# A transformer-gated recurrence on one core: four pieces of a hand-ordered slot change places

## What is computed

```python
x = L0_attn_x
xn = _layernorm(x, axis=-1)
s = recurrence(xn)                 # s_t = A s_{t-1} + B u_t, y = C s + D
g = _silu(_L0_ffn_ref(xn, ...))
return x + s * g

# in _L0_ffn_ref, DEPTH = 6 times:
x = attn_layer(shift_tokens(x), Wqkv[i], q_scale[i], k_scale[i], Wo[i]) + x
x = ffn_layer(shift_tokens(x), ln_g[i], ln_b[i], W1[i], b1[i], W2[i], b2[i]) + x
# attn_layer: 16 heads of 64, q and k l2-normalised and rotated,
# softmax over a local window of 32 (64 keys a query), then Wo
# ffn_layer: layernorm, W1, a * gelu(gate), W2
```

## Time and profile before

| | |
|---|---|
| median of 3 runs | 1641.66 us (1640.87 to 1642.63) |
| the profiled execution, its own time | 1641.48 us |
| its span | 1639.7 us |
| TensorE busy | 1575.6 us, 96% |
| VectorE busy | 1418.0 us, 86% |
| GpSimd busy | 1233.6 us, 75% |
| ScalarE busy | 1113.4 us, 68% |

### The profile page before, as it was taken

One profiled execution on the slowest core, in us unless ns is written; L12 is line 12 of the kernel. 1 busy time (PEld: TensorE's weight loads), 2 busy tenths in 40 slices (PEclk: granted clock), 3 DMA queues, 4 the chain that ended last, 5 costly groups with the idle time before them and its releaser, 6 DMA issues.

```text
span 1639.7 us, 75430 instructions
## 1 busy us (share of the span) xinstructions
PE 1575.6 (96%) x31996; PEld 1314.5 (80%) x31996; DVE 1418.0 (86%) x2750; ACT 1113.4 (68%) x1989; POOL 1233.6 (75%) x1200
## 2 busy tenths in 40 slices
PE   6889999999999999999999999999999999999997
PEld 3577888888888888888888888788888878888885
DVE  5798988898899889889988988998889889888963
ACT  4356667766776777676777767776676676667764
POOL 2677877887787878777887777787778887877851
PEclk9899999999999999999999999999999999999998
DMA  3232223333223333322333322333323333322231
GB/s 113 65 73 69 69 69 96 78 84 83 69 69 80 92 79 78 74 70 68 99 75 85 80 69 67 95 80 79 84 66 73 80 92 77 84 71 69 68 100 51
DMA packets 111326, 127.96 MB, mean 78 GB/s; under 512 B 52112, under 2 KB 57744, under 8 KB 110736
## 3 DMA queue, kind: packets, MB, share of 16 engines
q1 hardware_dynamic: 110992, 123.13, 29.8%
HBM read 20.27 MB, written 2.10 MB: 14 GB/s over the span
## 4 chain that ended last, share of the span: by engine, by line
PE 69%; DVE 11%; ACT 10%; issue 6%; SPq 1%; POOL 1%; DMA 1%; POOLq 0%; DVEq 0%; ACTq 0%
PE F L548 10%; PE O L654 10%; PE VTb L569 7%; PE S L605 7%; PE QKb L519 7%; PE F L638 4%; PE QKb L521 4%; PE QKb L520 4%; PE S L617 4%; DVE t L912 3%; ACT L813 3%; PE S L519 2%; PE S L521 2%; DVE mx L923 2%; PE S L520 2%
## 5 line engine op out<-in xcount | busy, mean ns | idle before, releaser
L1087 POOL TENSOR_TENSOR t<-t 128x512 f32<-128x512 f32 x384 | 492.6, 1283 | 188.6 <-DVE t L912 175.4
L1062 POOL TENSOR_TENSOR t<-t,rn 128x512 f32<-128x512 f32 x384 | 402.1, 1047 | 137.2 <-DVE rn L976 137.1
L912 DVE TENSOR_TENSOR t<-QKb,table 128x1024 f32<-128x1024 f32 x384 | 468.7, 1221 | 38.1 <-ACT sq L742 35.0
L742 ACT ACTIVATE sq<-QKb 128x512 f32<-128x512 f32 x384 | 231.7, 603 | 266.1 <-PE QKb L521 266.1
L654 PEld LDWEIGHTS O<-PT,V 64*64 64x64 f32 x12288 | 198.3, 134 | 58.2 <-issue 57.4
L654 PE MATMUL O<-PT,V 64*64 64x32 f32 x12288 | 218.3, 220 | 16.4 <-DVE rn L976 15.9
L936 DVE TENSOR_REDUCE ss<-sq 128x16 f32<-128x1024 f32 x192 | 232.0, 1209 | 0.0
L569 PE MATMUL VTb<-cst,t 128*128 128x128 f32 x1536 | 230.3, 272 | 0.9 <-ACT QT L759 0.7
L548 PEld LDWEIGHTS F<-wo_sb,OT 128*128 128x128 f32 x1536 | 200.2, 191 | 16.6
L1080 POOL TENSOR_TENSOR E<-E,rs 128x512 f32<-128x512 f32 x192 | 200.6, 1045 | 13.3 <-DVE rs L947 13.3
L569 PEld LDWEIGHTS VTb<-cst,t 128*128 128x128 f32 x1536 | 185.3, 141 | 30.9 <-issue 5.4
(11 more groups left out here) (142 smaller groups left out, 2775.4 us busy)
## 6 DMA issues: line engine op xcount, KB each, us to landing
V<-v_tok SPq DMA_DIRECT2D x1440, 64.0 KB, 2.0
w_raw<-in_wqkv SPq DMA_DIRECT2D x36, 256.0 KB, 3.2
wo_sb<-in_wo SPq DMA_DIRECT2D x6, 512.0 KB, 3.9
xs<-xm SPq DMA_DIRECT2D x48, 64.0 KB
xs<-xm SPq DMA_DIRECT2D x48, 63.5 KB
w_sb<-in_w SPq DMA_DIRECT2D x6, 341.0 KB, 4.5
w_sb<-in_w SPq DMA_DIRECT2D x6, 192.0 KB, 3.6
V<-in_x SPq DMA_DIRECT2D x4, 256.0 KB, 3.5
```

Source lines behind the costliest of these rows:

```text
L742: act.activation(sq[:, v % 4, :], QK_ps, ACT.Square).then_inc(sq_done, 1)
L912: dve.tensor_tensor(t12[:, v:9 + v % 4:8 + v % 4 - v, :].rearrange("p c (h d) -> p c h d", h=8), QK_ps.rearrange("p (h d) -> p h d", h=8). ...
L1062: pool.tensor_tensor(w, w, rn[:, vv // 4, 8 * (vv % 4):8 * (vv % 4 + 1)].unsqueeze(2) .to_broadcast([P, 8, DH]), ALU.mult).then_inc(qk_nor ...
L1087: pool.tensor_tensor(w, w, t12[:, 8 + v % 4, :].rearrange("p (h c d) -> p h c d", h=8, c=2)[:, :, ::-1, :], ALU.add).then_inc(add_done, 1)
```

## The change

Pieces change places in the blocks of four engines, and AFF's lag goes from 30 to 29. What is computed, the tiles, the transfers and the number of instructions stay. The core of the diff, each piece cut to its place:

```diff
-F_WO, F_MID, F_SH, F_ST, F_NM, F_XT, F_AFF = 21, 24, 25, 27, 28, 30, 30
+F_WO, F_MID, F_SH, F_ST, F_NM, F_XT, F_AFF = 21, 24, 25, 27, 28, 30, 29
...
                         project(QK_ps, par, tile, QK_COLS[2 * half + kind]).then_inc(qk_ready, 1)
 
+                    f, pr = batch(s, par, v, F_XT)
+                    if f is not None:
+                        wait(pe, normed, (f + 1) * NT)
...
+                            mm = pe.transpose(BANK_XT[:, P * t:P * (t + 1)], xn[:, t, :], ident)
+                        mm.then_inc(xnT_ready, 1)
+                    recurrence(in_fill(s, v, 0))
+
                     for k in range(QPS):
                         f, pr = batch(s, par, v, F_WO + k)
...
+                    if v == TX and live(s + 1, STEPS):
+
+                        wait(act, tx_ready, s + 1)
...
+                        stage(BANK_TX[:, 0:N], 1 - par)
                     u, vv, st, pr = unit(s, par, v, L_V)
...
+                    a, k, st, pr = quad(s, par, v, L_NORM)
+                    if live(a, QUADS):
+                        wait(pool, rs_done, a + 1)
...
                     u, vv, st, pr = unit(s, par, v, L_SCALE)
                     if live(u, UNITS):
...
+                    if live(g, UNITS):
+                        wait(pool, t12_done, g + 1)
...
+                                           ALU.add).then_inc(add_done, 1)
...
                     f, pr = batch(s, par, v, F_NM)
                     if f is not None:
                         wait(pool, ln2_done, (f + 1) * NT)
...
-                    a, k, st, pr = quad(s, par, v, L_NORM)
```

More of the change, by code:

```diff
@@ L552, in step @@
                                 mm.then_inc(wo_ready, 1)
[L554 to L562, removed]
                     u, vv, st, pr = unit(s, par, v, L_TR)
@@ L590, in step @@
                     recurrence(in_fill(s, v, 1))
+                    a, k, st, pr = quad(s, par, v, L_PT)
+                    if live(a, QUADS):
+                        wait(pe, p_norm, a + 1)
+                        wait(pe, sub_done, upto(a + 2, QUADS))
+                        wait(pe, pt_evac, a)
+                        for ct in range(4):
+                            mm = pe.transpose(PT_ps[:, P * ct:P * (ct + 1)], E[:, k, P * ct:P * (ct + 1)], ident)
+                        mm.then_inc(pt_ready, 1)
                     a, k, st, pr = quad(s, par, v, L_S)
@@ L609, in step @@
                         mm.then_inc(s_ready, 1)
[L611 to L618, removed]
+                    f, pr = batch(s, par, v, F_HID)
+                    if f is not None:
+                        ff_w1(f, pr, [2])
                     f, pr = batch(s, par, v, F_W1)
@@ L889, in step @@
                     g = s * SLOTS + v
+                    f, pr = batch(s, par, v, F_HID)
+                    if f is not None:
+                        hidden(f, pr, [0, 1])
                     f, pr = batch(s, par, v, F_END)
@@ L892, in step @@
                         finish(f, pr)
[L893 to L898, removed]
                     recurrence(in_fill(s, v, 0))
@@ L904, in step @@
                                           ALU.add).then_inc(mid_done, 1)
+                    f, pr = batch(s, par, v, F_W2)
+                    if f is not None:
+                        hidden(f, pr, [2])
                     if live(g, UNITS):
@@ L930, in step @@
                                           ALU.subtract).then_inc(sub_done, 1)
[L931 to L956, removed]
                     u, vv, st, pr = unit(s, par, v, L_NEWTON)
@@ L977, in step @@
                                                      op1=ALU.mult).then_inc(nw_seq, 1)
+                    f, pr = batch(s, par, v, F_ST)
+                    if f is not None:
+                        wait(dve, xs_moved, 48 * (f + 1))
+                        for t in range(NT):
+                            dve.bn_stats(ln6[:, t, :], xs[:, t, :]).then_inc(ln6_done, 1)
+                        wait(dve, normed, f * NT)
+                        for t in range(NT):
+                            wait(dve, ln6_done, f * NT + t + 1)
+                            dve.bn_aggr(ln2[:, t, :], ln6[:, t, :]).then_inc(ln2_done, 1)
+                    u, vv, st, pr = unit(s, par, v, L_SS)
+                    if live(u, UNITS) and vv % 2 == 0:
+                        wait(dve, sq_done, u + 2)
+                        dve.tensor_reduce(ss[:, vv // 4, 8 * (vv % 4):8 * (vv % 4) + 16],
+                                          sq[:, vv % 4:vv % 4 + 2, :].rearrange("p a (h d) -> p (a h) d", h=8),
+                                          AX_X, ALU.add).then_inc(ss_done, 1)
+                    a, k, st, pr = quad(s, par, v, L_EXP)
+                    if live(a, QUADS):
+                        wait(dve, exp_done, a + 1)
+                        dve.tensor_reduce(sm[:, k, :], E[:, k, :].rearrange("p (c k) -> p c k", k=KEYS), AX_X, ALU.add)\
+                           .then_inc(sum_done, 1)
+                        wait(dve, sum_done, a + 1)
+                        wait(dve, p_norm, a - 3)
+                        dve.reciprocal(rs[:, k, :], sm[:, k, :]).then_inc(rs_done, 1)
                     if v == TX and live(s + 1, STEPS):
@@ L1063, in step @@
                                            .to_broadcast([P, 8, DH]), ALU.mult).then_inc(qk_norm, 1)
+                    for l, c in splits(s, v, b_, SPLIT):
+                        split_weights(l, c)
+                    if live(g, UNITS):
+                        wait(pool, t12_done, g + 1)
+                        w = t12[:, v, :].rearrange("p (h c d) -> p h c d", h=8, c=2)
+                        pool.tensor_tensor(w, w, t12[:, 8 + v % 4, :].rearrange("p (h c d) -> p h c d", h=8, c=2)[:, :, ::-1, :],
+                                           ALU.add).then_inc(add_done, 1)
+                    if s == 0 and v in (3, 5):
+                        split_weights(0, 3 + v // 2)
                     f, pr = batch(s, par, v, F_NM)
```

18 lines of the change are left out of this document (10 added, 8 removed).

## The result

The changed kernel takes 1653.01 us (median of 4 runs, 1652.55 to 1654.69), the kernel before 1641.26 us beside it (4 runs, 1639.34 to 1642.63). The ratio is 1.0073, 95% interval 1.0058 to 1.0087: 11.8 us more, where 9.5 were forecast. The changed kernel's profiled execution has a span of 1652.9 us against 1639.7, at a granted clock of 0.99 of full speed in both.

A forecast was written before the change was run, and what follows sets the result against it. TensorE's queue was taken to bound the kernel. On 1641.48 us, 6.1 us for ordinary steps and 3.4 for the splitting steps made 9.5, giving 1651.0 us, 0.6% slower, with a range of 1643.5 to 1657.5.

The forecast's parts named there:

- Items 1 and 2: TensorE's XT ahead of WO in slot 6, and ScalarE's AFF at the end of slot 5: cost 0 each.
- Item 3: ScalarE, slot 4, x_hi ahead of v_tok: v_tok under 0.8 us later, cost 0; 0.8 us a step without cover.
- Item 4: GpSimd's NORM ahead of SCALE, NM behind add(4): scale(5) delays slot 6's VTb transposes 0.18 us, 34 steps, 6.1 us.
- the w_lo figure: TensorE's 0.05 us release after GpSimd's w_lo; as lower bound for slot 6's transposes, 0.09 a step, 3.1 us.
- the covered case: Rival, chance 0.13: slot 6's transposes lose nothing in ordinary steps, only the splitting steps cost, 2.5 us: 1644.0.
- The splitting steps: Five steps splitting value weights in slot 5: w_lo ends later, V(6) starts 0.67 us later, 3.4 us in sum.
- The end of a layer: Last step of the first five layers: W1(0)'s idle time swallows the lateness, cost 0 if the table ends as before.
- The third rival: VectorE's table misses its gap at layer ends, five times 1.0 us on top of the sum: 1656.0; chance 0.10.
- the forecast case: GpSimd's moves cost 6.1 us in ordinary steps and 3.4 in splitting steps, spanning 1648 to 1655; chance 0.63.
- Its transposes a slot later still start on time: Slots 1, 3 and 7: SCALE comes 1.0 us later behind NORM, and the transposes following it are not delayed.
- Slot 2's stall: TensorE's wait before slot 2's value product for VectorE's Newton steps, 15.9 us in all: to stay at 47 times.
- no gain came by t12(7): Rival, chance 0.06: without AFF there, VectorE's slot 7 product starts 0.11 us sooner, 47 times, 5.2 us faster: 1636.3.

The follow-up runs named there:

- experiment 5: The change, with GpSimd's scale(5) also moved behind add(5) in steps that split no weights in slot 5; 1695.04 us, ratio 1.0336.
- experiment 10: The kernel before, with only XT ahead of WO on TensorE and AFF at the end of slot 5 on ScalarE; 1638.49 us, ratio 1.0000.
- experiment 4: The change, with TensorE's XT put back behind WO; 1651.95 us, ratio 1.0077.
- experiment 9: The kernel before, with only ScalarE's casts to x_hi moved ahead of v_tok in slot 4; 1640.91 us, ratio 1.0013.
- experiment 11: The change, with ScalarE's v_tok put back ahead of x_hi; 1652.79 us, ratio 1.0084.
- experiment 1: The change, with GpSimd's order of NORM, SCALE, NM and add put back as before; 1640.47 us, ratio 1.0008.
- experiment 2: The kernel before, with only GpSimd's NM moved behind the add of slot 4; 1647.10 us, ratio 1.0053.
- experiment 3: The kernel before, with only GpSimd's NORM moved ahead of SCALE in odd slots; 1642.16 us, ratio 1.0019.
- experiment 6: The change, with VectorE's two table instructions moved behind the residual add of slot 0; 1646.93 us, ratio 1.0043.
- experiment 7: The kernel before, with the tables behind the residual add and the w_lo for slot 6 ahead of NORM; 1635.61 us, ratio 0.9964.
- experiment 8: The change, with GpSimd's w_lo split of slot 5 moved ahead of NORM and SCALE in five steps; 1658.68 us, ratio 1.0112.

## Why the prediction was right, and where it was off

**What bounds the kernel** held: experiment 5 made TR(6) wait 1.25 us longer than the change does and the kernel grew by 43 us over the change.

**Items 1 and 2** held (experiments 10 and 4), with the cover of 0.8 us at the place named.

**Item 3, "Cost 0", was wrong** for the move by itself: 2.3 us by the trace of experiment 9, 2.1 by its time (0.5 to 3.6). The step looked for who waits for v_tok's bank and for the V transfers, and rightly found nobody; the loss is not a wait but 0.10 us inside TensorE's score block. In the change it is hidden behind GpSimd (experiment 11), so it added nothing to the sum.

**Item 4, the ordinary steps**, was right in mechanism and too large in size: 4.7 us against 6.1. scale(5)'s end was forecast to 0.01 us. Of the 0.18 us a step, 0.14 was the release, taken from the QT copy; it measured 0.05 to 0.07, the w_lo figure that I had kept as the lower bound. What brings the loss up to 0.14 is a part that the sum did not have: transposes that start right at their release take 0.65 us where the four took 0.60, and V(6) comes 0.04 to 0.05 us later for it (1.4 to 1.8 us in sum). Experiments 1, 2 and 3 show that it takes both moves. The sign that was to show the covered case, TR(6) 1.1 us behind XT's start with no gap, was badly chosen: it is there in the change, though the wait is not covered. In the change the late score block of item 3 hides it; in experiment 11, without that, the distance is mostly 1.21 us.

**The splitting steps** measured 3.4 us against 3.4 forecast, 0.64 to 0.74 each for a forecast 0.67.

**The end of a layer, "Cost 0, if the table ends when it did", was the step that failed.** The first table instruction was to slip in ahead of add(7). It missed that gap and the next one. VectorE's timeline of the change, cut to a window in which only the first of the two ends:

```profile
800.77 2.97 DVE L884 TENSOR_TENSOR table<-cst,scales 128x256 f32<-128x256 f32 x1
```

It was asked for in scale(7), and was held over add(7) and scale(0) too. All five pairs took 3.19 to 3.31 us (2.08 to 2.71 before). The third rival, to which I gave 0.10, priced this at 1.0 us each; it measured 4.2 us for the five. So the forecast case and this rival came together: 4.7 + 3.4 + 4.2 = 12.3 us by the trace, 11.8 by the runs, 13.2 by the spans. That 9.5 lies as near to 11.8 as it does is in part luck: the ordinary steps were put 1.4 us too high, which made up for a third of the missing 4.2. Experiments 6 and 7 show the table's part from the other side: with the residual add ahead of it, W1(0) has no idle time.

**"Its transposes a slot later still start on time"** (item 4, for slots 1, 3 and 7) failed at the same place. GpSimd is not one instruction later there: scale(7) ends 1.4 to 1.95 us later against TR(7) than before, and TR(0) waits for it in all five. The table hides this in the change; experiment 6 leaves it open, 0.3 us a layer.

What decides whether a table instruction gets its gap stays open. In the first experiment the pair starts in add(7) and gets in between add(7) and scale(0); in the change and in experiment 4 it starts 0.58 to 0.73 us into scale(7) and misses in all cases; in experiments 2 and 3 it missed in four of five. The moment of its start does not decide alone. In the change and then in experiment 5, VectorE's tables at the end of the fourth layer:

```profile
1061.49 3.31 DVE L884 TENSOR_TENSOR table<-cst,scales 128x256 f32<-128x256 f32 x2
```

```profile
1088.92 2.17 DVE L884 TENSOR_TENSOR table<-cst,scales 128x256 f32<-128x256 f32 x2
```

Both start 0.58 us behind the start of scale(7) (1060.91 and 1088.34) and have the same instructions beside them; the second got in before add(7). So did two more of the ten pairs of experiments 5 and 8, at 0.58 and 0.59, while others there at 0.59 to 0.62 missed.

**Slot 2's stall** stayed at 47 times, as said, and no gain came by t12(7).

## What to carry to other kernels

For an instruction that moves on an engine off the critical path, write down its reader's due time and its own new end; the cost is what the end lies behind, and two moves that are free one by one can cross it together. A free slot is spent once: in the change scale(5) has nothing in hand, and whatever goes ahead of it, with all that this itself waits for, is paid in full (1.2 to 2.5 us a step in experiment 8). A VectorE instruction with two SBUF inputs that meets a busy GpSimd belongs behind whatever others are waiting for.

## What the runs showed of the hardware

A VectorE instruction with two SBUF inputs waited for three GpSimd instructions in a row and took 2.97 us, where the pair takes 0.75 us with GpSimd idle. The Trainium skill says that the first to issue holds the port for its whole instruction and the other blocks ("SBUF — State Buffer", Who interferes with whom). The rows agree that it blocks; they add that GpSimd's next instruction, which starts later than VectorE's recorded start, can go first, twice; in other pairs with the same start it did not.

TensorE started its weight load 0.05 to 0.06 us after GpSimd's recorded end, in the change and in experiments 5 and 11 alike (TR(6) mostly 0.05 to 0.07 us after it).

The 64 small matmuls of a score block took 0.96 instead of 0.86 us after a change in the order of two ScalarE pieces in the slot before. The cause is not known.
